# Graph attention behind a layer norm on one core: centring x inside the transpose, scaling behind the product with W, a turned f1, a reordered prologue

## The reference

```
h  = relu((x - mean) / sqrt(var + 1e-5))          # per row of x
Wh = h @ W ;  f1 = Wh @ a1 ;  f2 = Wh @ a2
e  = leaky_relu(f1[i] + f2[j], 0.2), -9e15 where adj is 0
attention = softmax of e over i (axis 1)
out = x + elu(attention @ Wh)
```

## Time and profile before

| | us |
|---|---|
| median of 3 runs | 1141.4 (1138.89 to 1145.42) |
| profiled execution | 1151.24, its span 1149.5 |
| PE busy | 972.7 (85%) |
| DVE busy | 1014.1 (88%) |
| ACT busy | 955.6 (83%) |
| POOL busy | 573.9 (50%) |
| mean granted TensorE clock | 0.973 of full speed |

### The profile page before, as it was taken

How to read it: one execution, slowest core, us unless ns; L and a number is a source line. 1 busy time by engine, 2 the same in 40 slices (tenths; PEclk the granted TensorE clock), 3 DMA queues, 4 the chain that set the end, 5 groups by cost and what they waited for, 6 DMA issues and landing times.

```text
span 1149.5 us, 24207 instructions
## 1 busy us (share of the span) xinstructions
PE 972.7 (85%) x8960; PEld 834.0 (73%) x8960; DVE 1014.1 (88%) x1551; ACT 955.6 (83%) x1590; POOL 573.9 (50%) x316
## 2 busy tenths in 40 slices
PE   2647789888998899988998899888989899778887
PEld 1325578777887787777887778777878788667776
DVE  3238999899999999999999999899999999789973
ACT  1219889888999899988999999888989899778874
POOL 1214444365654555465655565456554656454444
PEclk9868999999999999999999999999999999999999
DMA  4245666677766667767676678766675767555614
GB/s 137 61 79 141 170 164 175 188 195 192 188 181 182 167 176 211 202 186 196 179 185 174 168 192 212 186 187 184 174 186 143 206 198 193 149 162 162 189 35 136
DMA packets 341525, 195.10 MB, mean 170 GB/s; under 512 B 25632, under 2 KB 337184, under 8 KB 341408
## 3 DMA queue, kind: packets, MB, share of 16 engines
q1 hardware_dynamic: 341408, 193.56, 62.6%
HBM read 176.69 MB, written 16.84 MB: 168 GB/s over the span
## 4 chain that ended last, share of the span: by engine, by line
issue 29%; DVE 29%; PE 18%; DMA 16%; POOL 6%; ACT 2%; SPq 0%; DVEq 0%; POOLq 0%; ACTq 0%
DMA f_scratch<-f 9%; DVE stored L558 7%; DVE neg L518 7%; DVE direct L553 6%; POOL direct L622 3%; PE tp L313 3%; DMA f_row<-f_scratch 3%; DMA raw<-in_adj 3%; PE acc_st L337 2%; PE acc_st L336 2%; PE acc_st L338 2%; PE acc L354 2%; PE acc L356 2%; PE acc L358 2%; POOL y L640 2%
## 5 line engine op out<-in xcount | busy, mean ns | idle before, releaser
L622 POOL TENSOR_SCALAR direct<-prob,inv 128x1024 f16<-128x1024 f32 x128 | 364.2, 2845 | 430.5 <-DVE inv L545 430.5
L530 DVE CUSTOM_DVE_ANT_0 prob<-tp,f_row 128x2048 f32<-128x2048 bf16 x128 | 293.4, 2292 | 20.0 <-DMA f_row<-f_scratch 11.8
L354 PE MATMUL acc<-v,direct 128*128 128x256 f16 x1024 | 280.4, 274 | 7.2 <-DVE direct L553 7.2
L356 PE MATMUL acc<-v,direct 128*128 128x256 f16 x1024 | 280.3, 274 | 0.0
L358 PE MATMUL acc<-v,direct 128*128 128x256 f16 x1024 | 280.1, 274 | 0.0
L336 PE MATMUL acc_st<-v,stored 128*128 128x256 f16 x992 | 272.8, 275 | 0.0
L337 PE MATMUL acc_st<-v,stored 128*128 128x256 f16 x992 | 272.8, 275 | 0.0
L338 PE MATMUL acc_st<-v,stored 128*128 128x256 f16 x992 | 272.7, 275 | 0.0
L400 ACT ACTIVATE prob<-prob,shift 128x2048 f32<-128x2048 f32 x128 | 256.5, 2004 | 11.0 <-issue 0.7
L393 ACT ACTIVATE prob<-prob,f 128x2048 f32<-128x2048 f32 x128 | 255.0, 1992 | 0.0
L313 PE MATMUL tp<-ident_b,neg 128*128 128x128 bf16 x2048 | 137.3, 221 | 122.9 <-DVE top L530 116.8
(11 more groups left out here) (64 smaller groups left out, 1176.1 us busy)
## 6 DMA issues: line engine op xcount, KB each, us to landing
raw<-in_adj SPq DMA_DIRECT2D x128, 1024.0 KB, 7.0
x_in<-in_x SPq DMA_DIRECT2D x128, 128.0 KB, 6.8
y<-in_x SPq DMA_DIRECT2D x128, 128.0 KB, 4.4
out<-y SPq DMA_DIRECT2D x128, 128.0 KB, 4.0
f_row<-f_scratch SPq DMA_DIRECT2D x32, 256.0 KB, 5.0
f_scratch<-f SPq DMA_DIRECT2D x32, 2.0 KB
prob<-in_W SPq DMA_DIRECT2D x1, 256.0 KB, 3.3
prob<-in_a SPq DMA_DIRECT2D x1, 256.0 KB, 4.5
```

The source lines that it names most:

```text
L354: nc.tensor.matmul(acc[:, m, :], p_d[:, 0, rows], v_c[:, 0, :], start=(j == 0 and m % 2 == 0), stop=False, skip_group_check=True)
L356: nc.tensor.matmul(acc[:, m, :], p_d[:, 0, rows], v_c[:, 1, :], start=False, stop=False, skip_group_check=True)
L530: nc.vector.tensor_tensor_reduce(out=prob[:, c % 2, :], in0=tp_b, in1=f1_row[:, b % 2, :], scale=1.0, scalar=-3.0e38, op0=ALU.add, op1=ALU ...
L622: nc.gpsimd.tensor_scalar(direct[:, c % 2, 0, :], p[:, 0:HALF], k, None, ALU.mult).then_inc(hi_direct, 1)
```

## The change

The prologue and the x path:

- PE makes (x - mean) transposed: per half of x one matmul with the identity and one with the mean, broadcast, against minus the identity, both f32 and into one PSUM accumulation. `normalise` and `make_offset` are gone.
- relu and the product with W work on centred, unscaled x. The inverse deviation multiplies f (line 380's successor) and, times W's scale, both parts of v. `w_cat` holds W as it is.
- f1 is collected in columns 0 to 3 of 32-column blocks; DVE turns a block, and four DMAs write rows of 32 values. The read comes an iteration later in SP's order, the outputs two iterations after their finish.
- W's largest value goes over a PE transpose, a DVE maximum and a PE matmul with ones. The sums of W times a are made by ACT. The first raw loads are issued at s = -16 and -10.
- POOL's product is a tensor_tensor with the scale broadcast. `take_direct` works in two halves. DVE's order in an iteration is changed, POOL adds outputs an iteration later. RX is 8 (7), RE 4 (3).

```diff
 def transpose_x(c):
-    pe.wait_ge(xn_ready, c + 1)
+    pe.wait_ge(mv_s, c + 1)
...
     for k in range(KC):
-        last = nc.tensor.transpose(xt_bank(c)[:, k * P:(k + 1) * P], xn[:, c % 2, k * P:(k + 1) * P],
-                                   ident[:])
+        columns = xt_bank(c)[:, k * P:(k + 1) * P]
+        nc.tensor.matmul(columns, x_in[:, c % RX, k * P:(k + 1) * P], ident[:], start=True, stop=False)
+        last = nc.tensor.matmul(columns, mv[:, c % RS, 0:1].to_broadcast([P, P]), minus_ident[:],
+                                start=False, stop=True)
...
 def split_v_high(c):
+    act.wait_ge(k_row_s, c // 4 + 1)
-    nc.scalar.copy(v[:, c % RV, 0, :], wh_bank(c)[:, 0:FO]).then_inc(v_hi, 1)
+    nc.scalar.activation(v[:, c % RV, 0, :], wh_bank(c)[:, 0:FO], ACT.Copy, scale=k_row[:, c % RS:c % RS + 1]
+                         ).then_inc(v_hi, 1)
...
 def split_v_low(c):
-    nc.vector.tensor_tensor(v[:, c % RV, 1, :], wh_bank(c)[:, 0:FO], v[:, c % RV, 0, :], ALU.subtract
-                            ).then_inc(v_ready, 1)
+    nc.vector.scalar_tensor_tensor(out=v[:, c % RV, 1, :], in0=wh_bank(c)[:, 0:FO],
+                                   scalar=k_row[:, c % RS:c % RS + 1],
+                                   in1=v[:, c % RV, 0, :], op0=ALU.mult, op1=ALU.subtract
...
+def turn_f1(piece):
+    dve.wait_ge(f_ready, 4 * piece + 4)
+    wait(dve, f1_written, 64 * (piece - 1))
+    nc.vector.transpose(f1_t[:, piece % 2, :], f12[:, 32 * (piece % 2):32 * (piece % 2) + 32]
+                        ).then_inc(f1_turned, 1)
...
 def write_f1(piece):
-    sp.wait_ge(f_ready, 4 * piece + 4)
+    sp.wait_ge(f1_turned, piece + 1)
...
+    rows = f1_dram[b, 512 * q:512 * (q + 1)].rearrange("(c g r) -> g c r", g=4, r=32)
+    for g in range(4):
+        sp.dma_start(rows[g], f1_t[32 * g:32 * g + 4, piece % 2, :]).then_inc(f1_written, 16)
...
 # split_high, POOL
-nc.gpsimd.tensor_scalar(direct[:, c % 2, 0, :], p[:, 0:HALF], k, None, ALU.mult
+nc.gpsimd.tensor_tensor(direct[:, c % 2, 0, :], p[:, 0:HALF], k.to_broadcast([P, HALF]), ALU.mult
...
 # DVE, one iteration
     mask_scores(s); statistics(s + 23); split_v_low(s + LEAD)
+    add_halves(block of s - 1)
     aggregate(s + 23); add_eps, every fourth
-    finish_elu(finish of s - 1)
+    turn_f1, every fourth
     split_low(s - 1)
-    make_offset, every fourth
-    add_halves(block of s)
+    scale_rows, every fourth
     make_mask(s + 2)
+    finish_elu(finish of s - 1)
     reciprocal(s); scale_inverse(s)
```

More of the change, by code:

```diff
@@ L264, in _ @@
                     load_x(s + 25)
-                if chunk(s + LEAD) and (s + LEAD) % 4 == 3:
-                    write_f1((s + LEAD) // 4)
+                if chunk(s + LEAD - 1) and (s + LEAD - 1) % 4 == 3:
+                    read_f1((s + LEAD - 1) // 4)
                 for k in finish(s + 1):
@@ L270, in _ @@
                     sp.dma_start(y[:, k % RY, :], x[bo, rows, :]).then_inc(x_res_in[k % RY], 16)
-                if chunk(s + LEAD) and (s + LEAD) % 4 == 3:
-                    read_f1((s + LEAD) // 4)
-                for k in finish(s - 1):
+                for k in finish(s - 2):
                     sp.wait_ge(y_ready, k + 1)
@@ L276, in _ @@
                     sp.dma_start(out[bo, rows, :], y[:, k % RY, :]).then_inc(y_out[k % RY], 16)
+                if chunk(s + LEAD) and (s + LEAD) % 4 == 3:
+                    write_f1((s + LEAD) // 4)
             for i in range(RY):
@@ L314, in transpose_mask, with spread_max_w @@
                 last.then_inc(tp_ready, 1)
+            def spread_max_w():
+                pe.wait_ge(w_max, 1)
+                nc.tensor.transpose(max_t, tops[:, 0:1], ident[:]).then_inc(w_max_t, 1)
+                pe.wait_ge(w_max_one, 1)
+                nc.tensor.matmul(max_all, ones, tops[0:1, 1:2], start=True, stop=True).then_inc(w_max_all, 1)
             def store_block(n):
@@ L352, in direct_blocks @@
                 for m in range(NB):
+                    if j == 0 and m % 4 == 0:
+                        wait(pe, z_direct_ready, 2 * b - 1 + m // 4)
                     rows = slice(m * P, (m + 1) * P)
@@ L584, in _ @@
                     split_v_low(s + LEAD)
+                n = block_at(s - 1)
+                if n is not None and not first_half(n):
+                    add_halves(n)
                 if chunk(s + 23):
@@ L588, in _ @@
                     add_eps((s + 23) // 4)
+                if s == -20:
+                    multiply_w()
+                if chunk(s + LEAD) and (s + LEAD) % 4 == 3:
+                    turn_f1((s + LEAD) // 4)
+                if chunk(s - 1):
+                    split_low(s - 1)
+                if s == -20:
+                    largest_w()
+                    largest_of_all()
+                    scale_w()
+                if chunk(s + 23) and (s + 23) % 4 == 3:
+                    scale_rows((s + 23) // 4)
+                if chunk(s + 2):
+                    make_mask(s + 2)
                 for k in finish(s - 1):
                     finish_elu(k)
-                if chunk(s - 1):
-                    split_low(s - 1)
-                if chunk(s + 23) and (s + 23) % 4 == 3:
-                    make_offset((s + 23) // 4)
-                n = block_at(s)
-                if n is not None and not first_half(n):
-                    add_halves(n)
-                if chunk(s + 2):
-                    make_mask(s + 2)
                 if chunk(s):
```

180 lines of the change are left out of this document (101 added, 79 removed).

## The result

The kernel after takes 1149.43 us (median of 11 runs, 1148.85 to 1149.67), the kernel before 1141.4 beside it. The ratio is 1.0072, 95% interval 1.0055 to 1.0089: slower by 0.7%. The forecast was 1114, and "faster" with a chance of 0.69. The profiled execution's span is 1147.9 us (1149.5 before). The one of the kernel before was a long execution, 9.8 us over its median, so a sum over the two traces comes out 1.6 us lower where the medians are 8.0 us higher.

A forecast was written before the change was run, and what follows sets the result against it. DVE was taken as the bound, 8.03 us an iteration without a gap, PE having 0.8 us left. Terms -11-12.5+10-13-2 = -28.5 took 1151.2 to 1122.7; less 9.8 for the median, 1113, written as 1114; range 1088 to 1160.

The forecast's parts named there:

- rival A: PE's weight loads for the x matmuls don't hide, 0.19 us a record: +30 us, about 1171; chance 0.16.
- C: Rival in which POOL's product gets slower; chance 0.12.
- DVE order: Addition of halves before the split, elu last, POOL's output additions an iteration later: between 0.47 us and none saved.
- The sum: Main part set by the slower loop, PE 7.95 or DVE 8.0 us; all terms together -28.5 us.
- x centred by PE: On PE, eight matmul records of 0.12 us replace two transposes per chunk: +0.75 us, PE's iteration 7.95.
- POOL's product: The tensor_scalar of 2.85 us becomes a tensor_tensor with a broadcast operand, taken at 2.9 us: no change.
- The output additions: POOL's additions come right behind its product and mostly miss DVE's low parts; each had cost DVE 0.47 us.
- f1 and the ends of batches: At batch ends, about 19 us over plain intervals; two thirds go, -13 us.
- Rival D: The four small writes of f1 take as long as the one: about 1132 us; chance 0.08.
- Prologue: Up to the first mask addition: -6-15+14-4, -11 us, bounds -22 and +3.
- The last batch: Without x work, the addition of halves hides behind POOL's product, elu loses that cover: -2 us.

The follow-up runs named there:

- e2: The kernel after with the addition of halves (block s - 1) moved ahead of DVE's low part of v: 1111.07 us, ratio 0.9723.
- e10: The kernel after with the x path of the kernel before: 1097.76 us, ratio 0.949.
- e4: The kernel before with the addition of halves (block s - 1) behind the low part of v: 1137.67 us, ratio 0.996.
- e1: The kernel after with the addition of halves (block s) back in its old place behind the split: 1142.46 us, ratio 0.9998.
- e6: e2 with the x path of the kernel before: 1078.86 us, ratio 0.9397.
- e8: e2 with the matmuls of the mean left out, so x is not centred: 1083.26 us, ratio 0.943.
- e3: The kernel before with POOL's product as a tensor_tensor with the scale broadcast: 1145.37 us, ratio 0.9971.
- e7: e2 with POOL's product as a tensor_scalar with a pointer, as before: 1121.97 us, ratio 0.9767.
- e12: The kernel before with f1 turned on DVE and written as 128-byte rows: 1118.12 us, ratio 0.9785.
- e9: e2 with the old f1 write, one DMA of 512 pieces of 4 bytes: 1175.21 us, ratio 1.016.
- e11: e6 with normalise moved from ACT to POOL in every iteration: 1082.32 us, ratio 0.9366.

## Why the prediction was wrong

**The failed step.** The time, 1149.43, lies in the range of 1088 to 1160, but only since that range had room for rival A (weight loads that don't hide) and for C (a slow product on POOL), and neither of them happened; the forecast's direction was wrong. The step that failed is in the part "DVE order": "The addition of halves goes before the split". I counted from it only what it brings (no meeting with POOL, and later a hidden place in the last batch) and did not ask who waits for it and what it now stands behind. It stands behind the low part of v, which waits for PE; PE's stored block waits for it. In "The sum" I took the slower of two loops, PE 7.95 and DVE 8.0, with both running free. They are one ring: 8.89 us, with 0.83 of PE idle. e2 undoes that one fault, and there the forecast's lengths stand: 8.17 with and 7.97 without against the 8.05 and 7.95 predicted. That its time comes so near as well, 1111.07 us against 1114, is in part luck: the prologue and the last batch gave some 20 us more than predicted, while the sum set out from a long execution of the kernel before. The same step costs 38 us in the kernel after, 17 to 19 where PE is short (e10) and nothing in the kernel before (e4). The intervals without an addition are at 8.14 in the kernel after and 7.97 in e1 and e2. The surplus is in the first two of the seven, the interval 8, where the last late addition stands (8.52 against 7.59 in e2), and the one behind it (8.59 against 8.36); from the third on the kernel after and e2 agree to 0.01 us.

**x centred by PE.** Eight records take 0.90 us (497.19 to 498.09), 0.112 each: the lower end, where 0.12 was taken. Rival A fell: the weight loads are 0.19 us long here too, and hide all the same:

```profile
L320 PEld LDWEIGHTS pre<-ident,x_in x476: 186/190/333, 15.0 to 981.8; 128*128 128x128 f32 x159
```

What the prediction missed is that the step was not worth its price: I priced PE's +0.75 at +10 us beside attention, the runs say 29 to 32 us in all (e2 against e6), since PE's length binds once the meeting on DVE is gone (e8). With the old x path the rest of the change is 5.1% faster than before as it stands (e10), and 6.0% with the addition first (e6).

**POOL's product** took 1.895 us, under the lower bound of 2.2 and far from the 2.9 taken; C, the slower product to which I gave a chance of 0.12, fell. It gave little, 4.5 us in the kernel before (e3) and 10 in e2 (e7), most of that where no x work is left: in mid-run POOL has 80 us of 125 idle. The form with two inputs, one of them broadcast, took 1.895 us and the one-input form 2.845 on the same shape and types.

**The output additions** no longer meet DVE's products, as predicted: low parts of 1290 and 1277 ns (1377 and 1591 before), 51 us of DVE's work. e3 and e7 show that the order did it.

**f1 and the ends of batches.** Predicted -13, measured 13 x -0.90 = -11.7, for the reason given: the write alone brings the same ends to the kernel before (8.04 in e12). Rival D fell. But the prediction read f1's price off DVE's 11.8 us of waiting; SP's 275.2 us show where it lay. The low clock at the ends went with the waits: where the kernel before has 0.53 of full speed, no 4 us of the kernel after between 80 and 1140 us have under 0.97. In the kernel before the write alone is worth 24.8 us (e12), and of its trace's gain 15.6 us are the prologue.

**Prologue.** -11 predicted, -20.6 measured, inside the bounds. The turned write gives 15.6 (e12). The new x path, which has +14 in my sum there, gives 3.8 (75.02 in e6, 71.25 in e2). No run shows the 14: the fifteen intervals behind the first f take 38.0 us with the new x path (e2) and 40.9 with the old one (e6), at a granted clock of 1.00 and 0.87. Its matmuls of the mean do cost 6.3 (e8), so about 10 come back; that they come from `normalise` and the wait for the inverse deviation is my reading, not shown by a run. The first f came at 15.42, 8.3 us earlier, where 6 was estimated.

**The last batch.** -2 predicted, -13.0 measured. The addition ahead of the split is the larger part (7.98 to 7.22 in e1 and the kernel after), the product some of it (7.61 in e7), and f1's write some at the end of batch 6 (8.03 to 7.68 in e12, 5.6 us); the three don't add up.

## What to carry to other kernels

When an instruction is moved on one engine, write down who waits for it and what the one in front of it waits for; if the way leads back to the same engine, add up the circle: here it was 8.89 us while PE was busy 117 of 125. Place work that another engine waits for into the gap ahead of a wait, not behind it. A scattered DMA of 2 KB cost 25 us here, since the one queue stood behind it (275.2 us in all, 31 times). And price work that moves by what its new engine will have left after the whole change: PE had 0.8 us left in an iteration before, and was the bound after.

## What the runs showed of the hardware

- One DMA of 512 pieces of 4 bytes took some 10 us (10.15 in the earlier trace rows, 9.8 from the write's issue to the read's in e9), and its harm depends on what SP has behind it: taking it away gave 25 us in the kernel before, putting it back cost 64 in e2 (50 by the ratios).
- A tensor_tensor with a broadcast operand, 128x1024 f32 to f16 on POOL, took 1.895 us, a tensor_scalar with a pointer 2.845, each in the old and the new order (e3 and e7).
- With POOL's tensor_scalar on x beside DVE's low parts (e11) it was mostly POOL's instruction that got long (up to 1804 ns, 555 in the median), while DVE's stored low part kept 1284 ns on average. In the kernel before POOL's output additions (up to 1807 ns) and DVE's low parts (1591 ns on average) were both long.
- f32 matmul records of 128 columns follow each other at 0.112 us in the kernel after, though their weight loads take 0.190 us.
